# Narrower token tiles for the remainder of each expert, and a second staging buffer for expert weights

## The reference

```python
logits = x @ router_weight.T                      # 8 experts, x has 4096 rows of 512
top_v, top_i = top_k(softmax(logits), 2)          # 2 experts for each token
top_v = top_v / top_v.sum(axis=-1, keepdims=True)
for e in range(8):                                # I_MOE = 352
    gu = x @ gate_up_proj[e].T
    gate, up = gu[:, :352], gu[:, 352:]
    out = out + (silu(gate) * up @ down_proj[e].T) * combine[:, e:e + 1]
out = out + sigmoid(x @ shared_gate_w.T) * shared # a dense expert of 1408 for every token
```

## Time and profile before

| what | value |
|---|---|
| median of the runs | 2299.63 us |
| the profiled execution | 2297.75 us, its span 2296.0 us |
| TensorE busy | 2140.8 us (93%) |
| VectorE, ScalarE, GpSimd busy | 1156.5, 732.5, 473.6 us |
| mean granted clock of TensorE | 0.969 |
| DMA, mean over the span | 100 GB/s |

### The profile page before, as it was taken

How to read it: one execution, slowest core, us unless ns; L and a number is a source line. 1 busy time by engine, 2 the same in 40 slices (tenths; PEclk the granted TensorE clock), 3 DMA queues, 4 the chain that set the end, 5 groups by cost and what they waited for, 6 DMA issues and landing times. The chain is left out here.

```text
span 2296.0 us, 33530 instructions
## 1 busy us (share of the span) xinstructions
PE 2140.8 (93%) x11910; PEld 1652.1 (72%) x11910; DVE 1156.5 (50%) x2233; ACT 732.5 (32%) x1273; POOL 473.6 (21%) x851
## 2 busy tenths in 40 slices
PE   6999999999999826999999999999999999999995
PEld 4666676666766525777777777778888888888884
DVE  4766857668576665444444444444424334334232
ACT  3434435344353321434433333432111111111111
POOL 2222414224142212111111111000120120220213
PEclk9999999999999956999999999999999999999998
DMA  6035141451413112444444444333120220210202
GB/s 178 30 102 151 55 131 54 113 148 56 131 50 100 56 75 93 149 148 148 153 157 165 157 176 149 137 110 115 37 91 18 73 91 18 73 62 31 90 19 92
DMA packets 106894, 228.78 MB, mean 100 GB/s; under 512 B 9664, under 2 KB 23744, under 8 KB 103648
## 3 DMA queue, kind: packets, MB, share of 16 engines
q1 hardware_dynamic: 94368, 187.28, 24.7%
q0 software_dynamic: 12480, 40.90, 6.0%
HBM read 160.52 MB, written 66.06 MB: 99 GB/s over the span
## 5 line engine op out<-in xcount | busy, mean ns | idle before, releaser
L1050 PE MATMUL ex_bank<-ex_xT,ex_gu 128*128 128x512 f32 (+1 forms) x1656 | 392.6, 395 | 1.5 <-DVE ex_xT L1084 1.5
L1050 PEld LDWEIGHTS ex_bank<-ex_xT,ex_gu 128*128 128x128 f32 (+1 forms) x1656 | 298.7, 180 | 87.8 <-issue 1.9
L1100 DVE TENSOR_TENSOR sh_silu<-sh_silu,sh_bank 128x512 f32<-128x512 f32 x88 | 60.6, 688 | 444.4 <-ACT sh_silu L1093 413.3
L749 ACT ACTIVATE at_PT<-at_bank 128x512 f32<-128x512 f32 (+1 forms) x384 | 187.8, 527 | 264.4 <-PE at_bank L455 258.2
L599 DVE TENSOR_REDUCE at_nmax<-at_bank 128x1 f32<-128x384 f32 (+3 forms) x512 | 217.2, 474 | 108.4 <-PE at_bank L403 108.3
L1050 PE MATMUL sh_bank<-sh_xT,sh_gate 128*128 128x512 f32 x1056 | 256.2, 392 | 4.1 <-DVE sh_xT L1084 4.1
L1062 PE MATMUL sh_bank<-sh_dn,sh_act 128*128 128x512 f32 x1056 | 255.1, 390 | 0.0
L1050 PE MATMUL sh_bank<-sh_xT,sh_up 128*128 128x512 f32 x1056 | 253.7, 389 | 0.0
L1093 ACT ACTIVATE sh_silu<-sh_bank 128x512 f32<-128x512 f32 x88 | 52.9, 601 | 585.9 <-PE sh_bank L1050 533.0
L809 POOL TENSOR_TENSOR at_minus_max<-idf,at_nmax 128x512 fp32r<-128x512 f32 x128 | 133.8, 1045 | 503.9 <-DVE at_nmax L599 485.6
L1050 PEld LDWEIGHTS sh_bank<-sh_xT,sh_gate 128*128 128x128 f32 x1056 | 199.7, 189 | 46.0 <-DVE sh_xT L1084 4.3
(11 more groups left out here) (207 smaller groups left out, 2883.1 us busy)
## 6 DMA issues: line engine op xcount, KB each, us to landing
...
```

Of the source, the lines that this page charges most:

```text
L749: nc.scalar.activation(PT[g % 2][:, h % HG, TFROM[tb]:TFROM[tb] + TW[tb]], T_ps[tb][:, 0:TW[tb]], ACT.Exp).then_inc(pt_ready, 1)
L1050: last = self.nc.tensor.matmul(self.gate_up_ps[c % 2][which][0:m, :], cols(i, k), self.xT[j][:, k, :], start=(step == 0), stop=(step == 3 ...
L1100: nc.vector.tensor_tensor(silu[c % 2][0:m, :], silu[c % 2][0:m, :], gate_up_ps[c % 2][1][0:m, :], ALU.mult).then_inc(s["product"], 1)
```

## The change

Slots now lie in 23 places: 16 of 512 slots and one each of 448, 384, 320, 256, 192, 128 and 64 (80 columns of 128 instead of 92). Each expert gets a whole place for each full 512 of its tokens. What is left of each expert (its rest) is sorted by size, and the largest rest takes the first place that is free, the next the next one. Routing computes this, and the column of each place, in place of the multiples of 512; GpSimd writes place_base and tile_place in single-column memsets. The turns go through the places in the order PLACE_OF: eight full ones in a loop of pairs, then written out 448, full, 64, full, 128, full, 192, full, 256, full, 320, full, 384, full, full. In a turn every operation on tokens has the place's width or its number of blocks; gathers, stores and transposes likewise. The functions high_x, low_x, gate_silu and gate_times_up take the width w in the same manner as gate_up.

The staging buffer for weights and its semaphore exist twice, by parity. SP loads the first two tiles' weights in routing, and in turn n those of tile n + 2, in the same place of its order as before. The pieces are split in the same turns and in the same order as before.

```diff
@@ -43,8 +43,36 @@
 TS = 512
 NTT = NB * QT
 
-NT = (2 * NB * S + E * (TS - 1)) // TS
-SC = NT * TS // P
+
+
+FULL = 2 * NB * S // TS
+PLACE_WIDTH = [TS] * FULL + [TS * (E - 1 - j) // E for j in range(E - 1)]
+PLACE_BLOCKS = [(w + P - 1) // P for w in PLACE_WIDTH]
+PLACE_COLUMN = [sum(PLACE_BLOCKS[:p]) for p in range(len(PLACE_WIDTH) + 1)]
+NT = len(PLACE_WIDTH)
+SC = PLACE_COLUMN[NT]
+
+
+LOOPED = 8
+PLACE_OF = [*range(LOOPED), FULL, 8, FULL + 6, 9, FULL + 5, 10, FULL + 4, 11, FULL + 3, 12, FULL + 2, 13, FULL + 1, 14, 15]
+WIDTH = [PLACE_WIDTH[p] for p in PLACE_OF]
+BLOCKS = [PLACE_BLOCKS[p] for p in PLACE_OF]
+BLOCKS_BEFORE = [sum(BLOCKS[:n]) for n in range(NT + 1)]
+
+
+def blocks_before(n):
+
+    return BLOCKS_BEFORE[n] if isinstance(n, int) else QT * n
+
+
+def width(n):
+    return WIDTH[n] if isinstance(n, int) else TS
+
+
+def blocks(n):
+    return BLOCKS[n] if isinstance(n, int) else QT
+
+
 PASSES = ((0, 0), (0, 1), (1, 0))
...
-            nc.gpsimd.iota(slots_before[:], [[TS, E]], base=0, channel_multiplier=0, allow_small_or_imprecise_dtypes=True)
-            nc.gpsimd.iota(tile_no[:], [[1, NT]], base=0, channel_multiplier=0, allow_small_or_imprecise_dtypes=True)
+            nc.gpsimd.iota(expert_no[:], [[1, E]], base=0, channel_multiplier=0, allow_small_or_imprecise_dtypes=True)
+            nc.gpsimd.iota(place_no[:], [[1, NT]], base=0, channel_multiplier=0, allow_small_or_imprecise_dtypes=True)
+            for p in range(NT):
+                nc.gpsimd.memset(place_base[:, p:p + 1], float(P * PLACE_COLUMN[p]))
+            for n in range(NT):
+                nc.gpsimd.memset(tile_place[:, n:n + 1], float(PLACE_OF[n]))
...
             for q in range(weights.WN):
-                weights.split_hi(0, 0, q)
+                weights.split_hi(1, 0, q)
         @block.sync
         def _(sp):
             sp.wait_ge(expert_ready, 1)
-            weights.load(sp, 0)
+            for n in range(2):
+                weights.load(sp, n, n)
...
 
-            steps.then_wait(nc.vector.tensor_tensor(over[:, 0:E, :], n_of.unsqueeze(2).to_broadcast([P, E, E]),
-                                                    slots_before[:].unsqueeze(1).to_broadcast([P, E, E]), ALU.is_gt))
-            steps.then_wait(nc.vector.tensor_reduce(tiles[0][:], over[:, 0:E, :], AX_X, ALU.add))
-            steps.then_wait(nc.vector.tensor_copy(base[:], tiles[0][:]))
+            def of_expert(ap):
+                return ap.unsqueeze(1).to_broadcast([P, NT, E])
+
+            steps.then_wait(nc.vector.tensor_copy(whole_i[:, 2, :], n_of))
+            nc.vector.tensor_scalar(whole_i[:, 0, :], whole_i[:, 2, :], TS.bit_length() - 1, None, ALU.logical_shift_right)
+            steps.then_wait(nc.vector.tensor_scalar(whole_i[:, 1, :], whole_i[:, 2, :], TS - 1, None, ALU.bitwise_and))
+            nc.vector.tensor_copy(ends[0][:], whole_i[:, 0, :])
+            steps.then_wait(nc.vector.tensor_copy(whole[:], whole_i[:, 0:2, :]))
+            steps.then_wait(nc.vector.scalar_tensor_tensor(out=key[:], in0=whole[:, 1, :], scalar=float(E), in1=first_place[:],
+                                                           op0=ALU.mult, op1=ALU.add))
             b, shift = 0, 1
             while shift < E:
-                nc.vector.tensor_copy(tiles[1 - b][:, 0:shift], tiles[b][:, 0:shift])
-                steps.then_wait(nc.vector.tensor_tensor(tiles[1 - b][:, shift:], tiles[b][:, shift:],
-                                                        tiles[b][:, 0:E - shift], ALU.add))
+                nc.vector.tensor_copy(ends[1 - b][:, 0:shift], ends[b][:, 0:shift])
+                steps.then_wait(nc.vector.tensor_tensor(ends[1 - b][:, shift:], ends[b][:, shift:],
+                                                        ends[b][:, 0:E - shift], ALU.add))
                 b, shift = 1 - b, 2 * shift
-            end = tiles[b]
-            steps.then_wait(nc.vector.tensor_tensor(over[:], tile_no[:].unsqueeze(2).to_broadcast([P, NT, E]),
-                                                    end[:].unsqueeze(1).to_broadcast([P, NT, E]), ALU.is_ge))
-            steps.then_wait(nc.vector.tensor_reduce(tile_e[:], over[:], AX_X, ALU.add))
+            end = ends[b]
+            nc.vector.tensor_tensor(first[:], end[:], whole[:, 0, :], ALU.subtract)
+            steps.then_wait(nc.vector.tensor_tensor(larger[:], key[:].unsqueeze(1).to_broadcast([P, E, E]),
+                                                    key[:].unsqueeze(2).to_broadcast([P, E, E]), ALU.is_gt))
+            steps.then_wait(nc.vector.tensor_reduce(rest_place[:], larger[:], AX_X, ALU.add))
+            steps.then_wait(nc.vector.tensor_scalar(rest_place[:], rest_place[:], end[:, E - 1:E], None, ALU.add))
+
+            of_tile = tile_place[:].unsqueeze(2).to_broadcast([P, NT, E])
+            nc.vector.tensor_tensor(over[0][:], of_tile, of_expert(first[:]), ALU.is_ge)
+            steps.then_wait(nc.vector.tensor_tensor(over[1][:], of_tile, of_expert(end[:]), ALU.is_ge))
+            steps.then_wait(nc.vector.tensor_tensor(over[0][:], over[0][:], over[1][:], ALU.subtract))
+            steps.then_wait(nc.vector.tensor_tensor(over[1][:], of_tile, of_expert(rest_place[:]), ALU.is_equal))
+            steps.then_wait(nc.vector.tensor_tensor(over[0][:], over[0][:], over[1][:], ALU.add))
+            steps.then_wait(nc.vector.tensor_tensor(over[0][:], over[0][:], of_expert(expert_no[:]), ALU.mult))
+            steps.then_wait(nc.vector.tensor_reduce(tile_e[:], over[0][:], AX_X, ALU.add))
             nc.vector.tensor_scalar(tile_expert[:], tile_e[0:1, :], float(E - 1), None, ALU.min).then_inc(expert_ready, 1)
 
-            steps.then_wait(nc.vector.tensor_tensor(base[:], end[:], base[:], ALU.subtract))
-            steps.then_wait(nc.vector.tensor_scalar(base[:], base[:], float(TS), None, ALU.mult))
+            steps.then_wait(nc.vector.tensor_tensor(at_place[:], rest_place[:].unsqueeze(2).to_broadcast([P, E, NT]),
+                                                    place_no[:].unsqueeze(1).to_broadcast([P, E, NT]), ALU.is_equal))
+            steps.then_wait(nc.vector.tensor_tensor(at_place[:], at_place[:],
+                                                    place_base[:].unsqueeze(1).to_broadcast([P, E, NT]), ALU.mult))
+            steps.then_wait(nc.vector.tensor_reduce(shift_rest[:], at_place[:], AX_X, ALU.add))
+            steps.then_wait(nc.vector.tensor_scalar(whole[:, 0, :], whole[:, 0, :], float(TS), None, ALU.mult))
+            steps.then_wait(nc.vector.tensor_tensor(shift_rest[:], shift_rest[:], whole[:, 0, :], ALU.subtract))
+            steps.then_wait(nc.vector.tensor_scalar(shift_whole[:], first[:], float(TS), None, ALU.mult))
+            steps.then_wait(nc.vector.tensor_tensor(shift_rest[:], shift_rest[:], shift_whole[:], ALU.subtract))
+
             steps.then_wait(nc.vector.tensor_tensor(t1[:], count[a][:], total[:], ALU.subtract))
-            steps.then_wait(nc.vector.tensor_tensor(t1[:], t1[:], over_tiles(base[:]), ALU.add))
             steps.then_wait(nc.vector.tensor_tensor(t1[:].rearrange("p t e -> p (t e)"),
                                                     t1[:].rearrange("p t e -> p (t e)"), rank_ps[:], ALU.add))
+            steps.then_wait(nc.vector.tensor_tensor(t2[:], t1[:], over_tiles(whole[:, 0, :]), ALU.is_ge))
+            steps.then_wait(nc.vector.tensor_tensor(t2[:], t2[:], over_tiles(shift_rest[:]), ALU.mult))
+            steps.then_wait(nc.vector.tensor_tensor(t1[:], t1[:], t2[:], ALU.add))
+            steps.then_wait(nc.vector.tensor_tensor(t1[:], t1[:], over_tiles(shift_whole[:]), ALU.add))
             for k in range(2):
...
-                    last = self.nc.tensor.matmul(self.gate_up_ps[c % 2][which][0:m, :], cols(i, k), self.xT[j][:, k, :],
+                    last = self.nc.tensor.matmul(self.gate_up_ps[c % 2][which][0:m, 0:w], cols(i, k), self.xT[j][:, k, 0:w],
...
+    def down(self, n, c, weights, tiles=QT, tiles_before=None):
         pe, m = self.pe, self.rows[c]
         if c == 0:
-            pe.wait_ge(self.s["out_taken"], QT * n)
+            pe.wait_ge(self.s["out_taken"], QT * n if tiles_before is None else tiles_before)
         pe.wait_ge(self.s["act_ready"], self.NC * n + c + 1)
-        for i in range(QT):
+        for i in range(tiles):
...
-        self.whole = [sb("gu_in", [P, C, 2 * I_MOE]), sb("dn_in", [P, self.NC, D])]
+        self.whole = [[sb(f"gu_in{r}", [P, C, 2 * I_MOE]), sb(f"dn_in{r}", [P, self.NC, D])] for r in range(2)]
...
-    def load(self, sp, n):
+    def load(self, sp, n, r):
...
-    def split_hi(self, n, r, q):
-        self.nc.scalar.wait_ge(self.loaded, 48 * n + 48)
-        self.nc.scalar.activation(self.piece(q, r, 0), self.piece(q), ACT.Copy).then_inc(self.hi, 1)
+    def split_hi(self, loads, r, q):
+        self.nc.scalar.wait_ge(self.loaded[r], 48 * loads)
+        self.nc.scalar.activation(self.piece(q, r, 0), self.piece(q, r), ACT.Copy).then_inc(self.hi, 1)
...
```

(73 more changed lines are left out.)

92 lines of the change are left out of this document (54 added, 38 removed).

## The result

| | before | after |
|---|---|---|
| median of the runs | 2300.16 us (2298.41 to 2301.14, 4 runs) | 2213.98 us (2211.64 to 2217.6, 4 runs) |
| profiled execution, its span | 2297.75, 2296.0 us | 2211.64, 2209.9 us |
| mean granted clock | 0.969 | 0.967 |
| routing | 62.9 us | 70.2 us |
| expert stage | 638.1 us | 545.1 us |

The change makes the kernel faster: the ratio of the medians is 0.9628 [0.9611, 0.9644]. The profiled executions differ by 86.1 us, of which the forecast named 79.9.

What follows compares the result with a forecast made beforehand. TensorE was taken to bound the expert stage, small VectorE steps routing. 614.8 - 77.6 + 2.9 + 5.4 + 6.4 = 551.9 us for the stage; with routing's 6.3 more, 2217.85 us profiled, 2219.7 us median; range 2204 to 2243.

Steps and rivals of the forecast that it cites:

- Widths and blocks: Expert stage: narrower products save 46.6 us, fewer down products 25.8 and fewer transposes 5.2, together 77.6 us of TensorE time.
- Late weights: Expert stage: with the second staging buffer weights arrive in time and 20.4 us of waits go (bounds 0 and 20.4).
- rival (c): Expert stage: weights stay late, as two loads share the engines with stores and gathers; 20.4 us stay, 2240 us; chance 0.09.
- Clean tiles: Expert stage: 23 undisturbed full tiles at 26.73 us each, 614.8 us, from which the sum starts.
- First tile cold: Start of the expert stage: the first tile starts at the lower clock, which costs 2.9 us.
- Waits behind narrow tiles: Ends of narrow tiles: TensorE waits for VectorE's work on the next tile's input, 5.4 us (bounds 0 and 8.8).
- The clock: 64-column tile: the clock falls some 5 us in and the next full tile starts cold, 6.4 us (bounds 0 and 13).
- (b): Rival, expert stage: the clock falls in the 64- and the 128-column tile; 2226 us; chance 0.20.
- (d): Rival, expert stage: several new waits per narrow tile together with (b); 2245 to 2295 us; chance 0.07.
- (e): Rival, expert stage: the clock falls in every narrow tile until the next full one is under way; 2328 us; chance 0.02.
- Routing: Routing, before the expert stage: more VectorE steps and GpSimd constants add 6.3 us, all exposed (bounds 4 and 10).

Runs made afterwards that it cites:

- The second profile of the changed kernel: The changed kernel run again unedited, on one chip with a kernel of further edits: 2213.23 us, 0.9619 of the kernel before.
- the padded kernel: The changed kernel with all 23 places 512 wide, keeping its second staging buffer, new routing and order: 2281.62 us, 0.9909 of the kernel before.

## Why the prediction was right, and where its sizes were off

**Widths and blocks (77.6): right.** In the kernel after, the narrow products stand 0.111 apart at 128 and 192 columns (first two chunks) and 0.119 at 256, 0.147 at 320, 0.175 at 384 and 0.203 at 448; the prediction took 0.111, 0.111, 0.125, 0.151, 0.178 and 0.205. By these spacings the products of the seven narrow tiles save some 1.3 us more than the 46.6 of the sum. The row of the 128-column tile above is half of what a full one costs, as the sum has it.

**Late weights (20.4): right, and right by its mechanism.** The wait on DMA vanished, and the kernel with only the second buffer has TensorE without a gap. The bound of zero gain, rival (c), fell with it. One reading was off without harm: the 12.3 us of the earlier trace rows count from the issue, and the tile in which the load is issued starts at 1036.77, so the weights are usable 15 us after it has begun and not 12. By its size the term was 21.9 rather than 20.4, since clean tiles are 613.3; the sum doesn't use it.

**Clean tiles (614.8): 1.5 too high.** The last tile makes no transposes and waits for no next input; 23 clean tiles are 613.3.

**First tile cold (2.9): wrong, by 2.8.** The prediction carried the cold start of the earlier trace rows over as a constant. In the profile after, the transposes ahead of it run at 0.50 and the clock rises before the first product:

```profile
894.22:897.80 3.58, 3.58 (x16) 3.27 (x16) 1.48 (x3) 1.79 (x3) 0.00 (x0) 0.50 0.98 363
897.95:899.35 1.40, 0.00 (x0) 0.00 (x0) 1.14 (x2) 1.38 (x2) 0.47 (x2) 1.00 0.07 26
```

The first tile takes 26.86, 0.13 over a clean one; in the other variants it takes 26.8 to 28.6. The rise came 3.7 us after the first transpose here (897.89 less 894.22). In the kernel before it came at 898.47, 11.4 us after the first transpose, which its timeline has here:

```profile
887.12 3.68 PE L1073 MATMUL ex_bank<-idf,ex_xg 128*128 128x128 f32 x16 [13.21 <-DMA ex_xg<-xn,ex_index]
```

In the thirteen profiles of this case the rise comes 2.9 to 4.0 us after the first transpose in seven and 8.3 to 11.4 us after it in six. What decides between these is not shown by the runs, and nothing in the trace before told that the changed kernel would fall among the seven.

**Waits behind narrow tiles (5.4): right in kind, 1.5 too high.** Four rows show this wait, 3.9 us in all: 1.70 behind the 128-column tile, as the 1.8 had it, but 0.88 behind the 64-column one, and 0.55 and 0.77 at two blocks against 0.8. Behind the tiles of three blocks there is none. In the sum this is hidden: 613.3 less 77.6, plus 0.1 and 4.0 of clock, is 539.8, and 545.1 were measured, so 5.3 remain. The 1.4 beyond the 3.9 are not idle time of TensorE, and no run takes them apart. That the total of this term comes out is luck. Placing narrow beside narrow took part of the waits away.

**The clock (6.4): right in place, 2.4 too high.** It fell in the tile where it was put, 4.1 us in, where the forecast had some 5. The term had two parts. The tile itself lasts 17.1, as forecast; against the 13.1 that the same tile takes at 128 columns this is 4.0 rather than 3.5. The other part, a cold start of the next full tile (2.9), did not come: the clock was back 2.8 us before it. Rivals (b), (d) and (e) price more falls. The second profile of the changed kernel shows one behind the 128 tile, the place that (b) names, but it costs 1.6 us and not the 6 of (b); no run with two buffers shows a fall within a narrow tile of 128 columns or more; where the clock fell there, it was at the start of the full tile behind.

The Trainium skill (TensorE: Matmul & The Clock Gate, section "HAM oscillation — how this bites in real kernels") describes thin matmuls whose short groups alternate with waits for DMA, so that the clock falls at each wait; it advises either an order of the loop with more products between such waits or padding to 512 and more. The prediction used the padding alone. The traces agree with that mechanism: with one buffer the narrow tiles hold waits of up to 10.14 us behind late weights, and the clock falls in six of the seven. In the changed kernel these waits are gone, and of its narrow tiles the 64-column one alone holds a fall. The pair with two buffers measures the padding: the padded kernel takes 2281.6 us, the thin one 2214.0, and each narrow tile, the 64-column one with its fall too (17.1), is shorter than a full one (26.73). Only the 64-column place gained by being wider, and by 128 columns.

**Routing (6.3): 1.0 too low.** 69.2 was the forecast, 70.2 came. VectorE's new block took 7.21 against 7.1:

```profile
844.87 0.17 DVE L1033 CAST ro_whole_i<-ro_count 128x8 int32<-128x8 f32 x1
...
852.08 0.43 DVE L1073 TENSOR_TENSOR ro_t<-ro_count,ro_total 128x256 f32<-128x256 f32 x1
```

The 46 constants took 1.7 rather than 1.3 (0.036 apart and not 0.03), and the first gather, 1.64 long here, some 0.5 more than before, for which the prediction had no term.

Together: 1.5 (last tile), 2.8 (cold start) and 2.4 (clock) too high, 1.0 (routing) too low, makes 5.7 of the 5.7 to 6.2 us by which median and profile lie below the forecast. Most of the gap is clock: cold starts were taken at their full size at two tiles, and neither came. In the second profile of this kernel some 3 us of it came back elsewhere, so a forecast of this kernel can't be held to less than that. The range's lower end, 2204, is 1.6 below what the terms named for it give (2213.3 less 5.4 and 2.3); nothing hangs on it.
